# First attention's head outputs with high and low keys-values side by side; type rows, joined last chunk, query units moved

## The reference

```python
# first attention (relu features), per head:
phi_q, phi_k = relu(q @ rf.T), relu(k @ rf.T)  # q, k scaled by 1/8; 12 heads of 64, 256 features
attn = phi_q @ (phi_k.T @ v) / 256             # then attn @ W_proj + b_proj
# graph stack
h = concat([x, node_emb[node_type]], axis=-1)  # 768 + 128 = 896 features, 3 node types
xw = einsum('nd,rde->rne', h, w_rel)           # three relations, 896 x 896
agg = segment_sum(xw[edge_type, src] * inv[dst, edge_type], dst)
h = relu(agg + h @ w_root + bias)              # first convolution: 896 outputs
```

## Time and profile before

| | |
|---|---|
| time of three executions | 2228.92, 2229.34, 2235.43 us (median 2229.34) |
| the profiled execution | 2230.74 us, span 2229.0 us, mean granted TensorE clock 0.954 |
| PE, busy share | 91% |
| PE weight loads | 86% |
| DVE | 59% |
| ACT | 42% |
| first attention, pairs | about 111 to 259 us |
| projection, counts | about 259 to 316 us |
| g1 | about 316 to 579 us |

### The profile page before, as it was taken

The page is one execution under the profiler, slowest core; times in us unless marked ns, Lnnn a source line. Parts: engine busy times, 40 slices in busy tenths (PEclk is TensorE's granted clock), DMA queues, the critical chain, the costliest instruction groups (busy, mean ns, idle before and its releaser), DMA issues. The chain is left out here.

```text
span 2229.0 us, 34175 instructions
## 1 busy us (share of the span) xinstructions
PE 2031.5 (91%) x13715; PEld 1919.2 (86%) x13715; DVE 1324.0 (59%) x1860; ACT 940.3 (42%) x1143; POOL 89.9 (4%) x70
## 2 busy tenths in 40 slices
PE   5899889999999999955899979799979999999996
PEld 4889779999999999955789879699968888888885
DVE  8455665333334343446456756553358888888886
ACT  6444411221211122111356633222247777777775
POOL 0000000000000000000001100000000100101001
PEclk9999989999999999977899978899989999999998
DMA  3311134211111121110210030412269999999997
GB/s 81 101 29 29 57 100 93 67 34 51 51 58 58 29 73 49 58 29 1 93 29 29 15 135 15 158 48 93 79 233 385 384 384 378 366 372 374 367 374 269
DMA packets 186156, 313.71 MB, mean 141 GB/s; under 512 B 12641, under 2 KB 86884, under 8 KB 185628
## 3 DMA queue, kind: packets, MB, share of 16 engines
q1 hardware_dynamic: 180956, 295.38, 38.0%
q0 software_dynamic: 4816, 16.62, 3.2%
q10 hardware_dynamic: 272, 0.07, 0.0%
HBM read 293.56 MB, written 20.40 MB: 141 GB/s over the span
## 5 line engine op out<-in xcount | busy, mean ns | idle before, releaser
L179 PE MATMUL psum<-re_whi,xt_sb 128*128 128x512 f32 (+1 forms) x1680 | 507.5, 377 | 1.5 <-DVE xt_sb L2794 1.5
L179 PE MATMUL psum<-ring_hi,xt_sb 128*128 128x256 f32 (+3 forms) x1980 | 369.1, 284 | 10.8 <-DVE m_v L694 3.9
L179 PEld LDWEIGHTS psum<-re_whi,xt_sb 128*128 128x128 f32 x1680 | 313.0, 189 | 47.0 <-issue 1.9
L2778 DVE TENSOR_TENSOR re_wlo<-moe_raw,re_whi 128x1536 fp32r<-128x1536 f32 x173 | 303.5, 1756 | 35.1 <-ACT re_whi L2732 34.4
L179 PEld LDWEIGHTS psum<-ring_hi,xt_sb 128*128 128x128 f32 (+1 forms) x1980 | 312.0, 190 | 12.0 <-issue 5.3
L179 PE MATMUL psum<-re_wlo,xt_sb 128*128 128x512 f32 (+1 forms) x840 | 313.2, 373 | 0.0
L2732 ACT ACTIVATE re_whi<-moe_raw 128x1536 fp32r<-128x1536 f32 x174 | 258.7, 1490 | 90.7 <-PE psum L179 86.7
L179 PE MATMUL psum<-ring_lo,xt_sb 128*128 128x256 f32 (+3 forms) x990 | 280.5, 283 | 0.0
L179 PEld LDWEIGHTS psum<-ring_lo,xt_sb 128*128 128x128 f32 (+1 forms) x990 | 188.1, 190 | 0.0
L179 PEld LDWEIGHTS psum<-re_wlo,xt_sb 128*128 128x128 f32 x840 | 158.9, 189 | 22.1
L128 ACT ACTIVATE ring_hi<-ring_raw 128x1536 fp32r<-128x1536 f32 (+2 forms) x67 | 102.2, 1526 | 159.8 <-PE psum L187 81.3
(11 more groups left out here) (400 smaller groups left out, 3288.5 us busy)
## 6 DMA issues: line engine op xcount, KB each, us to landing
moe_raw<-in_L_ffn_Wg_r SPq DMA_DIRECT2D x74, 768.0 KB, 9.0
moe_raw<-in_L_ffn_Wu_r SPq DMA_DIRECT2D x58, 768.0 KB, 8.4
moe_raw<-in_L_ffn_Wd_r SPq DMA_DIRECT2D x42, 768.0 KB, 6.2
re_more<-in_L_ffn_Wd_r SPq DMA_DIRECT2D x42, 768.0 KB, 9.4
re_more<-in_L_ffn_Wu_r SPq DMA_DIRECT2D x30, 768.0 KB, 7.8
ring_raw<-in_L_gnn_w_rel SPq DMA_DIRECT2D x18, 896.0 KB, 5.1
re_more<-in_L_ffn_Wg_r SPq DMA_DIRECT2D x15, 768.0 KB, 7.3
ring_raw<-in_L_mix_W_qkv SPq DMA_DIRECT2D x24, 384.0 KB, 4.4
```

The lines of the kernel that those rows point to most:

```text
L179: mm = pe.matmul(out, lhs[a], rhs[b], start=(first and i == 0), stop=(last and i == 2))
L2778: dve.tensor_tensor(wlo[:, i % RING, :], raw[i % RAWS], whi[:, i % RING, :].bitcast(F32), ALU.subtract)\
```

## The change

1. **First attention.** `kv[:, 0]` now holds, for each head, the high part at the head's own 64 columns and the low part at the other 64. `attend` makes for each head two features x two parts of the queries x two halves = 8 matmuls, 16 in all, into a pair of banks for each head (head 1 in `k.pair[1]`, head 0 in `k.pair[0]`): 64 of the output rows are the product with the high part, the other 64 that with the low part. (So low x low is computed too.) ACT copies one half of the rows to `at_f` (`at_out`), DVE adds the other (`num_f`), for each head. Since `k.pair[1]` also takes the keys projection, its first unit waits for `num_f` of the pair two before.
2. **Query units.** In the first attention units 6 to 8 all stand behind m = 1.
3. **Type rows.** The embedding is loaded transposed (128 x 3) and split into `k.emb` (35 columns: high at 0 to 2, low at 32 to 34). `k.kind_rows` has for each node a one at its type, in four groups of rows. In g1 PE multiplies each weight chunk's last 128 rows by `k.emb` (`embed_products`, two matmuls into bank 3), ACT and DVE put the high and low part in `ew`, and each Y tile and R product has one type-row matmul (two for R's halves) in place of the seventh block's three (six).
4. **Joined last chunk.** The 128-wide weights of relations 0 and 1 are one ring chunk and one Y job of 256 columns, those of relation 2 and the root another chunk. 14 ring chunks for 16.

The diff, cut to its core:

```diff
@@ phase_attend
         def num_pair(hd):
-            return k.pair[0] if hd == 0 else k.pair[3]
+            return k.pair[0] if hd == 0 else k.pair[3 if second else 1]
...
-                    if p >= 2:
+                    if p >= 2 and second:
                         pe.wait_ge(s["kv_f"], p - 1)
+                    elif p >= 2:
+                        pe.wait_ge(s["num_f"], 2 * (p - 2) + 1)
...
-                            pe.wait_ge(s["at_out"], p)
+                            pe.wait_ge(s["num_f"], 2 * p)
...
-                    if m < 3:
+                    if second and m < 3:
                         project_unit(p + 1, KD + m)
+                    elif m == 1:
+                        for u in range(KD, KD + 3):
+                            project_unit(p + 1, u)
...
+                        for b in range(2):
+                            for h in range(2):
+                                mm = pe.matmul(num_pair(hd)[:, h, 0:HN], kv[:, 0, m, :], phiq[:, m, b, h * HN:(h + 1) * HN],
+                                               start=(m == 2 * hd and b == 0), stop=(m == 2 * hd + 1 and b == 1))
...
-                    act.wait_ge(s["at_mm"], p + 1)
-                    act.activation(halves(at_f[:, p, :]), k.pair[0][:, :, 0:HN], ACT.Copy).then_inc(s["at_out"], 1)
+                    for n, hd in enumerate((1, 0)):
+                        act.wait_ge(s["at_mm"], 2 * p + n + 1)
+                        act.activation(halves(at_f[own(hd), p, :]), num_pair(hd)[other(hd), :, 0:HN], ACT.Copy)\
+                            .then_inc(s["at_out"], 1)
...
+                        ins = dve.tensor_tensor(kv[:, 0, ms, other(hd)], kvf[:, ms, own(hd)],
+                                                kv[:, 0, ms, own(hd)].bitcast(F32), ALU.subtract)
...
+                for n, hd in enumerate((1, 0) if not second else ()):
+                    at_part = halves(at_f[own(hd), p, :])
+                    dve.wait_ge(s["at_out"], 2 * p + n + 1)
+                    dve.tensor_tensor(at_part, num_pair(hd)[own(hd), :, 0:HN], at_part, ALU.add).then_inc(s["num_f"], 1)
@@ phase_project
-            sp.dma_start(emb_sb[:], node_emb).then_inc(s["emb_loaded"], 16)
+            sp.dma_start(emb_f[:], node_emb.rearrange("r e -> e r"), allow_slow_non_contiguous=True).then_inc(s["emb_loaded"], 16)
             sp.wait_ge(s["t_lo"], KD)
-            for r in range(RELS):
-                sp.dma_start(type_i[r:r + 1, :], node_type.rearrange("(a n) -> a n", a=1)).then_inc(s["emb_loaded"], 16)
+            sp.dma_start(type_i, node_type.partition_broadcast(P)).then_inc(s["types_loaded"], 16)
...
-                    if i == EMBED_AT:
-                        embed()
...
+                if t == 1:
+                    act.wait_ge(s["emb_loaded"], 16)
+                    act.wait_ge(s["emb_zero"], 1)
+                    act.activation(k.emb[:, 0:RELS], emb_f[:], ACT.Copy).then_inc(s["emb_hi"], 1)
@@ new, and phase_rgcn
+def rgcn_plan(d_out):
...
+        groups = [(0, 1), (2, 3)] if w == P else [(0,), (1,), (2,), (3,)]
...
+        order = (("Y", 0), ("Y", 2), ("G", 0), ("G", 1), ("R", 3), ("G", 2)) if w == P else \
+            (("Y", 0), ("Y", 1), ("G", 0), ("Y", 2), ("G", 1), ("R", 3), ("G", 2))
...
+            def embed_products(n):
+                w = st.chunks[n][1]
+                pe.wait_ge(*st.split(n))
+                if n >= 1:
+                    pe.wait_ge(s["ew_lo"], n)
+                for a, v in enumerate(st.views(n)):
+                    mm = pe.matmul(k.banks[3][0:EMB_ROWS, 0:w], k.emb[:], v[:, KD, :], start=(a == 0), stop=(a == 1))
+                mm.then_inc(s["ew_mm"], 1)
...
-                        for j in range(kt):
+                        for j in range(full):
...
+                        if layer == 0:
+                            pe.wait_ge(s["ew_lo"], n + 1)
+                            mm = pe.matmul(k.banks[i % 3][0:TS[t], 0:w], k.kind_rows[0:TYPE_ROWS, t * P:t * P + TS[t]],
+                                           ew[0:TYPE_ROWS, n % 2, off:off + w], start=False, stop=True)
                         mm.then_inc(s["y_mm"], 1)
+                        if t == EMBED_TILE and job in begins:
+                            embed_products(begins[job])
```

More of the change, by code:

```diff
@@ L656, in _ @@
                 act.wait_ge(s["kv_f"], p + 1)
-                act.activation(kv[:, 0, :, :], kvf[:], ACT.Copy).then_inc(s["kv_hi"], 1)
+                if second:
+                    ins = act.activation(kv[:, 0, :, :], kvf[:], ACT.Copy)
+                else:
+                    for hd in range(2):
+                        ms = slice(2 * hd, 2 * hd + 2)
+                        ins = act.activation(kv[:, 0, ms, own(hd)], kvf[:, ms, own(hd)], ACT.Copy)
+                ins.then_inc(s["kv_hi"], 1)
                 if p + 1 < PAIRS:
@@ L901, in _ @@
         def _(pe):
-            def embed():
-                pe.wait_ge(s["emb_made"], 1)
-                for h in range(2):
-                    mm = pe.matmul(k.pair[3][:, h, 0:HN], emb_sb[:], onehot[:, h * HN:(h + 1) * HN], start=True, stop=True)
-                mm.then_inc(s["emb_ready"], 1)
             def check():
@@ L1465, in _ @@
                     continue
-                for m in range(w // P):
+                for m in range(cuts[c][1] // P):
                     i = g_at[c, r] + m
@@ new lines, in _ @@
+                        wh = [v[:, :, cols] for v in st.views(n)]
+                        for j in range(full):
+                            mm = split_product_wide(pe, pair, [v[:, j, :] for v in wh],
+                                                    lambda b_, h: h_in(j)[:, b_, h * HN:(h + 1) * HN], j == 0, j == kt - 1)
+                        if layer == 0:
+                            pe.wait_ge(s["ew_lo"], n + 1)
+                            for h in range(2):
+                                mm = pe.matmul(pair[:, h, 0:HN], ew[0:TYPE_ROWS, n % 2, cols],
+                                               k.kind_rows[0:TYPE_ROWS, h * HN:(h + 1) * HN], start=False, stop=True)
@@ L1488, in _, with embed_high @@
                     mm.then_inc(s["g_mm"], 1)
+                    if kind == "R" and m == 0 and job in begins:
+                        embed_products(begins[job])
         @block.scalar
         def _(act):
+            def embed_high(n):
+                w = st.chunks[n][1]
+                if n == 0:
+                    act.wait_ge(s["ew_zero"], 1)
+                if n >= 2:
+                    act.wait_ge(*st.freed[n - 2])
+                act.wait_ge(s["ew_mm"], n + 1)
+                act.activation(ew[0:EMB_ROWS, n % 2, 0:w], k.banks[3][0:EMB_ROWS, 0:w], ACT.Copy).then_inc(s["ew_hi"], 1)
```

200 lines of the change are left out of this document (130 added, 70 removed).

## The result

The changed kernel takes 2204.09 us in the median of 4 runs (2199.72 to 2210.09), beside 2230.61 for the kernel before (2228.92 to 2235.43): ratio 0.9879, 95% interval 0.9851 to 0.9908. I had forecast 2203.0, in a range of 2196 to 2213. The profiled execution took 2204.53 us for a span of 2202.7, so 26.2 us less than the profiled one before, where my sum had 27.0.

What follows compares the result with a forecast made beforehand. TensorE was taken to bound all three phases, so a matmul removed is time unless before a wait. Attention 3.5, projection 1.3 and graph layer 22.2 sum to 27.0 us off: 2203 us forecast, range 2196 to 2213.

Steps and rivals of the forecast that it cites:

- Graph layer g1: Fewer Y and R matmuls, 8.3 and 4.1; last chunk, 12.8; less 2.6 embedding products and 0.35 at the start: 22.2 us.
- Projection: The four `embed` matmuls go where PE has no wait: 1.3 us gained, other engines' steps priced at zero.
- rival 4: Embedding's element-wise load holds ACT in the projection; free up to 12.4 us, at 46 us time is 2237; chance 0.04.
- Attention: First attention, six pairs: fewer `attend` matmuls and earlier `keys_values`, less new waits on DVE's add; 3.5 us gained.
- (a): First attention: `attend` falls from 24 to 16 matmuls, 1.17 us saved a pair.
- (b): First attention: query units behind m = 1 let `keys_values` start 0.83 us earlier in a pair.
- (c): Middle pairs: PE waits 1.6 us for DVE's add before the next keys unit; a pair gains 0.38, four pairs 1.5.
- (e): Last attention pair: shorter `kv` steps gain 0.4, `attend` 1.8, an add of 0.8 behind it; together 1.4 us.
- Rival 1: Clock falls in the new waits, four of 1.6 us and one of 1.9; all five cost 8.8, 2212; chance 0.14.
- Rival 2: First attention: the adds don't hold PE, so 6.5 us more gain, 2197; chance 0.10.
- rival 3: g1's last chunk: a 128-column matmul is paced by its columns; 1.8 us saved for 12.8, 2214; chance 0.02.

Runs made afterwards that it cites:

- copies first: Changed kernel with ACT's copies and DVE's adds in the first attention put ahead of the next pair's query split; 2199.77 us median.

## Why the prediction was right, and where it was not

**Graph layer g1, 22.2 predicted, 23.4 measured.** From the issue of `g_b` to the first copy of the next phase it is 314.94 to 559.35 now, and 316.23 to 584.00 before: 244.41 for 267.77. A whole column chunk went from 67.17 to 63.12, so 4.05 for my 3.79; the first gained 2.1 for my 1.5; the last 13.1, as I had it. The prices per matmul held: 0.118 for 256 columns, and 0.1116 for 128 (2.12 over 19), where I took 0.109. For the join the cause is shown, by the version without it (9.7 us). For the type rows it is read from the distance of the tiles (2.25 us for 2.48) and of the chunks; no run takes them out alone. The 81 ns that the Trainium skill gives for a sustained 128-column matmul ("TensorE: Matmul & The Clock Gate", Back-to-back issue gap) is not what these products take: 0.1116 us.

**Projection, 1.3 predicted, 1.6 measured** (ACT's first activation to `g_b`: 54.92 for 56.56). The embedding's load landed in 5.6 us, so rival 4 never came near its 12.4.

**Attention, 3.5 predicted, 0.5 in the two profiles (147.94 us for 148.42 from the first keys activation on), 1.5 to 2.2 with the clock held in the last pair.** The pieces of (a), (b) and (c) held: 1.19 us for `attend` (1.17), 0.72 for the query units (0.83), a wait of 1.59 (1.6). What they add up to did not. I counted in (c) from the start of `attend`, so the steps are told apart by the same cut:

| stretch | before | now | gain | predicted |
| --- | --- | --- | --- | --- |
| first keys activation to first `attend` | 22.64 | 21.95 | 0.69 | 0.83 |
| first to fifth `attend` | 99.26 | 98.84 | 0.42 | 1.52 |
| fifth to last `attend` | 20.23 | 21.48 | -1.25 | 0.2 |
| last `attend` to the projection | 6.29 | 5.67 | 0.62 | 1.0 |

The last column is my terms (b) for the first pair; four times 0.38; 0.4 for the `kv` steps less 0.2 of late DVE; and 1.8 less 0.8 for the add. Two steps failed, and one term was taken from a row at fallen clock. **The gain of a middle pair in (c)** was 0.11 us and not 0.38, 1.1 us in all. The next keys unit comes 4.55 us behind `attend` for 4.03, so 0.52 later and not 0.45; until m = 2 another 0.09 is lost (16.22 for 15.61); and from there to `keys_values` 0.74 is gained and not 0.83. These are several hand-overs, each dearer by less than 0.1 us than I had them; no run takes them apart. **In (e), the last pair,** I had PE's lateness right (0.17 us at the third key tile for my 0.2) and gave no value to the clock in the pause there, which I had not listed: since `attend` is shorter, it grew from 1.05 to 2.46 us, and the clock fell in it. With the pauses filled and the clock at 1.00 the same stretch takes 20.06 us, 0.17 less than before, where I had 0.2; without, 21.48. That is 1.4 us. The term is the 1.8 for the last `attend`, a third of 5.28. It fell again, and 1.47 was gained; with the clock held the eight matmuls are worth 1.2, and the copy and the add take nearly all of that back (4.45 us for 4.53 from the last `attend` on, less the filling and the fallen clock).

**Rival 1** was the right mechanism at the wrong pauses. My four new waits of 1.6 us never lowered the clock (1.00 in 161 to 186); the last pair's did, in the old attention as well. In the new one it costs 2.6 us (23.89 for 21.26), in the old one 1.8 in one profile (`attend` 5.28 for 3.52) and 7.7 to 8.4 in another (28.80 for 21.06 or 20.40). I had treated the one profile of before as the rule. (The 2.1 us pause that I named stands before the third key tile, not the second.) **Rival 2** was out by the 1.59, **rival 3** by the 2.12.

**The sum.** 0.5 + 1.6 + 23.4 = 25.5 us; the changed kernel's first pair started 0.8 later, and behind g1 it gained another 1.6, which makes the 26.3 between the spans. The last two have no cause in the change that I can show, nor have the 2 us above; the changed kernel's own runs lie 10 us apart. So the total of 26 for my 27 is in part luck: the attention fell 3.0 us short, and g1, the projection and what I can't explain made up for 2.3 of it.

## What to carry to other kernels

When a saving on the bound engine puts a new step of another engine on its path, look at the order of work on that other engine first: here 0.6 us of a 1.6 us wait was the length of the step, and moving the urgent step ahead of one that nobody was waiting for gave back 1.3 us a pair. Price the first and the last turn of a loop by themselves, since what covers a chain in the middle is missing there. And before a value is given to a pause in which the clock may fall, take a second profile of the same kernel, and of the kernel before: one does not tell a fixed cost from a draw.

## What the runs showed of the hardware

A fallen clock can stay down through back-to-back work. The forty matmuls of 130 columns took 8.63 us for 4.58 in four of the profiles, and in the version with copies first PE was busy in all of 240 to 250 and the clock 0.50 in all of it:

```profile
240.00:250.00 10.00, 10.00 (x46) 9.98 (x46) 2.43 (x3) 1.45 (x3) 0.00 (x0) 0.50 0.01 2
...
265.00:268.00 3.00, 3.00 (x27) 3.00 (x27) 2.48 (x5) 1.73 (x3) 0.27 (x1) 0.99 0.52 153
```

It was back within some 4 us of the start of the projection's 256-column products at 261.06. With the attention of before it came back during `attend`, in 265 to 266, which had begun at 260.12; what decides this no run here shows. Where the block of forty began at full clock it stayed there (4.58 us) in every profile.

Whether a pause of 2 us lowers the clock differs from execution to execution of one kernel: 0.50 to 0.69 in one profile of the changed kernel, 1.00 in the other, at the same place. It fell in twelve of thirteen profiles. The Trainium skill ("TensorE: Matmul & The Clock Gate", What's actually happening) says that the gate's own timing is not tied to the kernel's start, so that the point of change moves between runs; the two profiles are in keeping with that, though they don't show the gate's timing itself. And matmuls that nobody reads, 0.147 us each, earned their time in such pauses, as long as they ended before the wait did.
